# A two-layer transformer kernel on one core: layer 0's values in one visit a group, their parts one step later, rows' transposes behind the sixth scores

## The reference, cut to what matters

```python
x = x + tanh(g_xattn[0]) * L0_xattn(layernorm(x), ctx_768, ...)   # 16 heads x 64, 154 keys
x = x + tanh(g_ffn[0])   * L0_ffn(layernorm(x), ...)              # 8 experts, top 2
x = x + tanh(g_xattn[1]) * L1_xattn(layernorm(x), ctx_768, ...)   # 8 heads x 128, 308 keys
x = x + tanh(g_ffn[1])   * L1_ffn(layernorm(x), ...)              # coupling network

def _L0_xattn_ref(x, context, Wq, Wk, Wv, Wo, bo):
    q, k, v = heads(x @ Wq), heads(context @ Wk), heads(context @ Wv)
    attn = softmax(einsum('bqhd,bkhd->bhqk', q, k) * scale)
    out = einsum('bhqk,bkhd->bqhd', attn, v).reshape(B, Nq, h * dh)
    return out @ Wo + bo
```

## Time and profile before

| | us |
|---|---|
| median of 3 runs | 925.71 (923.45 to 928.28) |
| the profiled execution | 926.4 |
| its span in the trace | 924.6 |
| PE busy | 881.2 (95%) |
| DVE busy | 513.5 (56%) |
| ACT busy | 511.7 (55%) |
| POOL busy | 374.0 (40%) |

### The profile page before, as it was taken

How to read it: one execution, slowest core, us unless ns; L and a number is a source line. 1 busy time by engine, 2 the same in 40 slices (tenths; PEclk the granted TensorE clock), 3 DMA queues, 4 the chain that set the end, 5 groups by cost and what they waited for, 6 DMA issues and landing times.

```text
span 924.6 us, 20158 instructions
## 1 busy us (share of the span) xinstructions
PE 881.2 (95%) x6773; PEld 764.1 (83%) x6774; DVE 513.5 (56%) x1257; ACT 511.7 (55%) x1450; POOL 374.0 (40%) x530
## 2 busy tenths in 40 slices
PE   6989999999999999999999987999999999999996
PEld 4567777777777779999999986899999999987653
DVE  4534434444445764434434447877777776666466
ACT  4576777777775244443343462655655555552565
POOL 3173444444443234455454551534434443443000
PEclk9999999999999799999999998999999999999998
DMA  9000000420002466777777813000000000000002
GB/s 267 1 1 2 1 1 2 146 72 1 0 2 80 138 240 234 244 245 258 232 262 246 252 61 89 25 23 13 12 23 11 12 1 2 1 1 0 1 1 91
DMA packets 36673, 76.18 MB, mean 82 GB/s; under 512 B 4941, under 2 KB 22721, under 8 KB 36481
## 3 DMA queue, kind: packets, MB, share of 16 engines
q1 hardware_dynamic: 32865, 65.11, 21.6%
q0 software_dynamic: 3744, 10.23, 3.3%
HBM read 66.02 MB, written 9.31 MB: 81 GB/s over the span
## 4 chain that ended last, share of the span: by engine, by line
PE 88%; DVE 4%; DMA 3%; issue 2%; ACT 1%; POOL 1%; SPq 0%; DVEq 0%; POOLq 0%
PE banks L1542 14%; PE banks L546 14%; PE banks L548 13%; PE banks L547 13%; PE banks L584 8%; PE banks L595 7%; PE banks L574 5%; PE banks L444 3%; PE banks L1827 2%; PE banks L515 1%; PE banks L1838 1%; PE banks L1832 1%; PE banks L1820 1%; PE banks L1532 1%; DMA region_a<-in_L_ffn_b 1%
## 5 line engine op out<-in xcount | busy, mean ns | idle before, releaser
L1098 ACT ACTIVATE region_a<-banks,negmax 128x154 f32<-128x154 f32 (+1 forms) x384 | 161.7, 434 | 29.3 <-DVE negmax L890 26.6
L1542 PE MATMUL banks<-region_b,region_a 128*128 128x128 f32 x1248 | 146.7, 276 | 1.5 <-ACT region_b L1578 1.4
L1542 PEld LDWEIGHTS banks<-region_b,region_a 128*128 128x128 f32 x1248 | 142.7, 192 | 3.2 <-ACT region_b L1578 1.7
L1242 POOL TENSOR_TENSOR region_a<-region_a,recip 128x640 f32<-128x640 f32 x64 | 80.3, 1255 | 137.4 <-DVE recip L894 137.4
L1205 POOL TENSOR_TENSOR region_a<-region_a,recip 128x512 f32<-128x512 f32 x64 | 66.7, 1042 | 134.3 <-DVE recip L894 94.9
L890 DVE TENSOR_REDUCE negmax<-banks 128x4 f32<-128x616 f32 (+1 forms) x128 | 100.5, 785 | 26.9 <-PE banks L574 14.2
L1633 DVE SCALAR_TENSOR_TENSOR region_b<-banks,region_a,region_b 128x128 f32<-128x128 f32 x156 | 43.9, 343 | 106.7 <-PE banks L1542 99.6
L584 PE MATMUL banks<-ident,region_a 128*128 128x128 f32 x640 | 95.0, 279 | 3.2 <-DVE pT_low L901 1.6
L584 PEld LDWEIGHTS banks<-ident,region_a 128*128 128x128 f32 x640 | 72.5, 141 | 16.6 <-issue 11.6
L546 PE MATMUL banks<-xT_high,Wq_high 128*128 128x256 f32 x256 | 77.8, 304 | 4.1 <-DVE xT_low L882 2.1
L1080 ACT CAST pT_high<-banks 128x640 fp32r<-128x640 f32 x64 | 44.4, 694 | 64.9 <-PE banks L584 64.9
(11 more groups left out here) (293 smaller groups left out, 2344.5 us busy)
## 6 DMA issues: line engine op xcount, KB each, us to landing
region_a<-in_L_ffn_W SPq DMA_DIRECT2D x39, 1024.0 KB
W<-in_L_ffn_W SPq DMA_DIRECT2D x1, 4096.0 KB, 17.9
W<-y_rows SPq DMA_DIRECT2D x16, 256.0 KB, 2.8
out<-x SPq DMA_DIRECT2D x8, 256.0 KB, 2.2
x<-in_x SPq DMA_DIRECT2D x1, 1536.0 KB, 13.1
region_b<-in_L_xattn_Wq SPq DMA_DIRECT2D x1, 1024.0 KB, 8.7
region_b<-in_L_xattn_Wo SPq DMA_DIRECT2D x1, 1024.0 KB, 13.6
xn_rows<-region_b SPq DMA_DIRECT2D x1, 1024.0 KB, 4.4
```

The source lines that it names most:

```text
L1098: e = act.activation(into, source, ACT.Exp, bias=negmax[:, n % 2, u:u + 1], accum_out=sums[:, n % 2, u:u + 1])
L1242: pool.tensor_tensor(probs1[:, n % 2], probs1[:, n % 2], rc, ALU.mult).then_inc(sem("p_norm"), 1)
L1542: mm = pe.matmul(banks[:, 2 * r + part, m * P:(m + 1) * P], W1[r][:, k, cols], xgT[:, r, k, :], start=(k == 0), stop=(k == DK - 1))
```

## The change

It has four parts.

1. **Layer 0's values** are done for a whole group in even steps only, by the new `pe_group_values`: four halves as before and four **quarters**, which hold the remainders as 64 keys by 64 columns (rows 64u of the array, columns 64i) in place of the padded 128 by 64. The output lies in two banks, `o0_ps`, of which bank 5 also receives the fifth transpose. So the fifth transpose in odd steps waits for `o0_copied`, ScalarE's copy of the values. In an even step the values take the probabilities that were transposed in the same step, and wait for their copy (`pt2_high` of this step, before: of the step before).
2. **The parts of a group's output.** ScalarE copies the values to SBUF (`o0T`) in plain float32, at the place where it made the high part. VectorE makes the high part from `o0T` by a copy with a cast, a new instruction, and then subtracts, both in odd steps directly behind the next step's maxima; before, there was the subtraction alone, in even steps. `pe_pair_out` of layer 0 waits for the parts per two chunks.
3. **The rows' transposes** (`pe_pair_x`), in both layers, stand behind the next scores of step 6 instead of ahead of them. Their high part on ScalarE moves from the end of step 5 to the start of step 6, their low part on VectorE from step 5 to step 6, behind the maxima.
4. **`values(6)`** stands ahead of q(0) instead of behind it, in both layers.

```diff
+        def pe_group_values(pe, g, b):
+
+            V = V0[b].bitcast(F32)
+            for u in range(2):
+                for i in range(2):
+                    pe.matmul(o0_ps[64 * i:64 * i + 64, u, :], V[:, 2 * g + u, 128 * i:128 * i + 64], p0T[:, g % 2, 2 * u + i, :],
+                              start=True, stop=False)
+            for i in range(2):
+                for u in range(2):
+                    rows = slice(64 * u, 64 * u + 64)
+                    mm = pe.matmul(o0_ps[64 * i:64 * i + 64, u, :], V[rows, 2 * g + u, 192 + 64 * i:256 + 64 * i],
+                                   p0T[rows, g % 2, 4, :], start=False, stop=True)
+            mm.then_inc(sem("o2_ps"), 1)
...
             for m in range(5):
+                if m == 4 and groups_copied is not None:
+                    pe.wait_ge(sem("o0_copied"), groups_copied)
                 mm = pe.transpose(probsT_ps[:, m * P:(m + 1) * P], row[:, m * P:(m + 1) * P], ident[:])
...
             for c in chunks:
-                if c == NC - 2:
+                if L is L0 and r == 0 and c % 2 == 0:
+                    pe.wait_ge(sem("o2_sb"), groups_done - (NC - 2 - c) // 2)
+                if L is L1 and c == NC - 2:
                     pe.wait_ge(sem("o2_sb"), L.groups + groups_done)
...
                 def values(n):
                     s = 8 * i + n
+                    if L is L0:
+                        if n % 2 == 0 and not (first and n in (0, 2)):
+                            pe.wait_ge(sem(probs_turned), s)
+                            if not (first and n == 4):
+                                pe.wait_ge(sem("o0_copied"), group + n // 2 - 2)
+                            pe_group_values(pe, (n // 2 - 2) % 4, before if n < 3 else batch)
+                        return
...
                 values(5)
+
+                next_scores(6)
                 if not last:
...
                     pe_pair_x(pe, L)
-
-                next_scores(6)
                 transposes(6)
...
+                values(6)
                 if not last:
                     pe.wait_ge(sem("xt2_sb"), x0 + i + 2)
                     pe_pair_q(pe, L, 0)
-                values(6)
...
             def o_rest(g, group):
                 high, low = oT_parts[L.index]
                 part = slice(2 * g, 2 * g + 2)
+                if L is L0:
+                    dve.wait_ge(sem("o0_copied"), group + 1)
+                    dve.tensor_copy(high[:, part, :], o0T).then_inc(sem("o2_high"), 1)
                 dve.wait_ge(sem("o2_high"), g0 + group + 1)
-                dve.tensor_tensor(low[:, part, :], o_ps.rearrange("p (u n) -> p u n", u=2),
+                dve.tensor_tensor(low[:, part, :], o0T if L is L0 else o_ps.rearrange("p (u n) -> p u n", u=2),
                                   high[:, part, :].bitcast(F32), ALU.subtract).then_inc(sem("o2_sb"), 1)
...
                             row_max((n + 1) % 8, s + 1)
+                    if n == 6 and not last:
+                        pair_x_rest(i + 2)
                     if not (first and n == 0):
                         probsT_rest((n - 1) % 8, s - 1)
+                    if L is L0 and n % 2 == 1 and not (first and n in (1, 3)):
+                        o_rest((n // 2 - 2) % 4, 4 * i + n // 2 - 2)
...
             def o_high(g, group):
                 act.wait_ge(sem("o2_ps"), g0 + group + 1)
+                if L is L0:
+                    if not (isinstance(group, int) and group == 0):
+                        act.wait_ge(sem("o2_sb"), group)
+                    act.copy(o0T, o0_ps).then_inc(sem("o0_copied"), 1)
+                    return
```

More of the change, by code:

```diff
@@ L184, in flamingo @@
         p0T = reg_a.part(10 * PAIR, "p (q m n) -> p q m n", q=2, m=5)
+        reg_a.at += 3 * DC
+        o0T = reg_a.part(2 * PAIR, "p (u n) -> p u n", u=2)
+        assert reg_a.at <= P0_AT + 20 * PAIR
         reg_a.at = P0_AT + 20 * PAIR
@@ L360, in flamingo @@
         o_ps = banks[:, 6, :]
+        o0_ps = banks[:, 5:7, P:P + PAIR]
         misc_ps = banks[:, 7, :]
@@ L579, in pe_pair_scores, with pe_pair_probsT @@
             mm.then_inc(sem("s_ps"), 1)
-        def pe_pair_probsT(pe, L, n):
+        def pe_pair_probsT(pe, L, n, groups_copied=None):
             row = normed if L is L0 else probs_row[:, n % 2]
             for m in range(5):
+                if m == 4 and groups_copied is not None:
+                    pe.wait_ge(sem("o0_copied"), groups_copied)
                 mm = pe.transpose(probsT_ps[:, m * P:(m + 1) * P], row[:, m * P:(m + 1) * P], ident[:])
             mm.then_inc(sem("pt_ps"), 1)
+        def pe_group_values(pe, g, b):
[10 more added lines that the diff above has]
+            mm.then_inc(sem("o2_ps"), 1)
         def pe_pair_pv(pe, L, g, u, b):
             c = 2 * g + u
[L590 to L601, removed]
+            for i in range(3):
+                m = 3 * u + i if i < 2 else 2
+                mm = pe_split(pe, o_ps[:, u * PAIR:(u + 1) * PAIR], (V_high[:, c, i, :], V_low[:, c, i, :]),
+                              (pT_high[:, g % 2, m, :], pT_low[:, g % 2, m, :]), i == 0, i == 2)
             if u == 1:
@@ L665, in transposes @@
                             pe.wait_ge(sem(probs_turned), s - 1)
-                        pe_pair_probsT(pe, L, (n - 1) % 8)
+                        turned = L is L0 and n % 2 == 1 and not (first and n < 5)
+                        pe_pair_probsT(pe, L, (n - 1) % 8, 4 * i + n // 2 - 1 if turned else None)
                 def next_scores(n):
@@ L707, in emit @@
                             pe.wait_ge(sem("l1_low"), len(L1_PARTS))
-                    pe_pair_out(pe, L, 0, misc_ps, range(0, 4), None)
+                    pe_pair_out(pe, L, 0, misc_ps, range(0, 4), 4 * i)
                 values(2)
@@ L761, in pe_pairs @@
             pe.wait_ge(sem(probs_turned), STEPS - 1)
-            pe_pair_probsT(pe, L, 7)
+            pe_pair_probsT(pe, L, 7, GROUPS - 2 if L is L0 else None)
             if L is L0:
@@ L765, in pe_pairs @@
                 pe_rows(pe, 2)
-            pe_pair_pv(pe, L, 2, 1, b)
+            if L is L0:
+                pe.wait_ge(sem(probs_turned), STEPS)
+                pe_group_values(pe, 2, b)
+            else:
+                pe_pair_pv(pe, L, 2, 1, b)
             if L is L1:
@@ L772, in pe_pairs @@
             pe.wait_ge(sem(probs_turned), STEPS)
-            pe.wait_ge(sem("o2_sb"), g0 + GROUPS - 1)
-            for u in range(2):
-                pe_pair_pv(pe, L, 3, u, b)
+            if L is L0:
+                pe.wait_ge(sem("o0_copied"), GROUPS - 1)
+                pe_group_values(pe, 3, b)
+            else:
+                pe.wait_ge(sem("o2_sb"), g0 + GROUPS - 1)
+                for u in range(2):
+                    pe_pair_pv(pe, L, 3, u, b)
             if L is L1:
@@ L1011, in emit @@
                         add_y(dve, L, 2 * i + n // 2 - 3, n // 2 - 1, misc_ps[:, 0:D])
-                    if n == 5 and not last:
-                        pair_x_rest(i + 2)
                     if n > 5 and not last and L is L1:
                         pair_q_rest(4 * i + n - 1, n - 6)
-                    if n % 2 == 0 and not (first and n in (0, 2)):
+                    if L is L1 and n % 2 == 0 and not (first and n == 0 or first and n == 2):
                         o_rest((n // 2 - 2) % 4, 4 * i + n // 2 - 2)
@@ L1147, in emit @@
                     s = 8 * i + n
+                    if n == 6 and not last:
+                        x_high(i + 2)
                     if not (first and n == 0):
@@ L1153, in emit @@
                         pair_q_high(4 * i + n + 3, n + 2)
-                    if n == 5 and not last:
-                        x_high(i + 2)
                     if n > 5 and not last:
```

2 lines of the change are left out of this document (added).

## The result

The changed kernel takes 948.26 us (942.95 to 951.29, four runs) against 924.75 for the kernel before: the ratio is 1.0231, interval 1.0197 to 1.0265. It is slower by 2.3%, on the side that was forecast, and 11 us above the 937 given: outside the forecast's own 930 to 945 and inside the wide range of 919 to 949 by 0.7 us only. A second measurement of the same file, among the experiments, gave 943.79 against 926.04, 1.0194 (1.0161 to 1.0227). The profiled execution took 942.95, 16.6 more than that of before.

A forecast was written before the change was run, and what follows sets the result against it. TensorE was taken as the bound (busy 95% of the span). Terms -14.4 - 0.5 - 5.1 + 3.8 + 6.0 + 11.9 + 5.8 + 2.2 + 1.3 = +11.0 on 926.4 gave about 937 us; own range 930 to 945, wide 919 to 949.

The forecast's parts named there:

- values, 4 groups: Layer 0's values on TensorE: a group takes 1.98 us instead of 2.44, -14.4 us over 32 groups.
- (a): Layer 0, values(6) directly behind T(6) wait for ScalarE's copy of these transposes: +0.64 x 6 = +3.8 us.
- (b): Layer 0, T(7)'s fifth transpose waits for ScalarE's copy of the values, behind the q copy: +1.0 x 6 = +6.0 us.
- (c): Layer 0, step 3: chunk 6 of the rows' output waits for VectorE's parts: 1.7 x 7 pairs = +11.9 us.
- (d): Layer 0, step 5: rows' transposes wait for y_done, late on VectorE: +0.97 x 6 = +5.8 us.
- (e): Odd steps: q copies no longer covered between block and next scores: +0.18 at two places a pair, +2.2 us.
- -0.85 x 6 = -5.1: Layer 1: moved rows' transposes and values(6) save waits of 0.71 + 0.25, less 0.11 kept back, in us.
- the prediction's upper case: In (c), S being scores' start: blocked cast ends S+2.9, subtraction S+3.4 to 4.0; wait +1.4 to +2.0 us.
- The row at 43.94: Normalisation begun 0.08 ahead of GpSimd's product, taking 1.27 us against 0.38 alone; cited as evidence that GpSimd locks VectorE.
- rival one: VectorE is not held by GpSimd: (c) 0.85 x 7, (d) 0.15 x 6; 926 us, no change; chance 0.28.
- rival two: Parts in layer 0 are done when chunk 6 comes; (c) and (d) both gone gives 919 us; chance 0.10.
- rival three: Quarters run two at a time: values term +13.8 instead of -14.4; 965 or 951 us; chance 0.10.

The follow-up runs named there:

- the run with the copy first: Changed kernel with ScalarE's copy of layer 0's values ahead of the copy of q(0) in step 6: 940.45 us, ratio 1.0151.

## Why the prediction was right, and where not

What was right is the way it went: layer 0's values won almost what was worked out, the five waits named took more than that back, and the sum of a pair came out above zero. What a pair of layer 0 shows, term by term, is in the table. The measured sizes are those of the pair from 125.34 to 159.57: the interval between two neighbouring matmul starts of the trace, less the interval that the same kinds of neighbours have where nothing is waited for.

| term, us a pair of layer 0 | predicted | measured | worked out as |
|---|---|---|---|
| values, 4 groups | -1.80 | -1.68 | 4 x (2.44 - 2.02) |
| (a) values(6) behind T(6) | +0.64 | +0.61 | 1.05 - 0.20, less the 0.24 for xT_low that went |
| (b) T(7)'s fifth transpose | +1.0 | +0.89 | 1.00 - 0.11 |
| (c) chunk 6 in step 3 | +1.7 | +1.43 | 1.55 - 0.12 |
| (d) y_done | +0.97 | +0.62 | 0.84 - 0.22 |
| (e) q copies | +0.37 | +0.23 | one place in place of two: 0.24 + 0.22 - 0.03 - 0.20 |
| transposes of step 2, behind GpSimd | none | +0.16 | 0.38 - 0.22 |
| rows' transposes, other changes of shape | -0.09 | +0.02 | the rest |
| whole pair | +2.8 | +2.28 | 34.23 - 31.95 |

The row that I had not listed is the contention's other side: GpSimd's slowed products end late, and the next transposes wait for them. No row shows the 0.09 that the prediction allows for a semaphore; in (a) the copy ends at 127.27 and the values start at 127.32, so 0.05. The layer's seven intervals are 13.7 longer; its terms came to 16.1 with the first pair and the tail.

**The term that failed is layer 1**, "-0.85 x 6 = -5.1". It counted the two waits that go, for x and for xT_low, and kept back 0.11 as a choice for what comes late. What comes late is a whole chain: values(6), moved ahead of q(0), no longer lies between q(0) and the scores that need it. One pair after the change:

```profile
670.72 0.58 ACT L1109 CAST q_high<-banks 128x512 fp32r<-128x512 f32 x1 [0.83 <-PE banks L552]
```

```profile
671.33 0.69 DVE L906 TENSOR_TENSOR q_low<-banks,q_high 128x512 fp32r<-128x512 f32 x1 [1.18 <-ACT q_high L1109]
```

```profile
672.08 0.41 PE L550 MATMUL banks<-K_high,q_high 128*128 128x308 f32 x1 [0.85 <-DVE q_low L906]
```

High part, low part, 0.85 idle on PE. In layer 0 I had asked what comes late behind q(0) (terms (b) and (e)); in layer 1 not. With 0 in its place the sum is +16.1, so 942.5 on the scale of the profiled execution, which took 942.95. That this is so close is partly luck: layer 0's terms were some 2 too large together, and layer 1's last pair, which had no wait for x to win, lost 0.75, and the clock around the experts and at the end adds a few us of either sign. The median of the first measurement is 5 us above its own profiled run, and the three runs above it have lower mean clocks (0.975 to 0.982 against 0.985); the second measurement's median is 1 below its profiled run. So these 5 go with the clock of that set of executions and with no step of the argument.

**Inside (c) the size was nearly right and its parts were not.** I had the cast blocked by the product until S+2.9 and the subtraction slowed a little. The cast began 0.08 ahead of the product and took 0.42, its time alone by the prediction's lower bound; the subtraction took twice its time, 1.41 for 0.69. The parts are ready at S+3.4 (112.31 to 115.73), the near end of the prediction's upper case, so the size came out by another way than the one forecast, and that is luck in part. The row at 43.94, on which I had put the block, also began 0.08 ahead of a product and was held; the casts that began so were not.

Of the Trainium skill's rule ("SBUF — State Buffer", Who interferes with whom) this case shows both halves. On two SBUF inputs: the subtraction takes 0.693 apart from GpSimd and 1.41 behind its product; with one input in PSUM, before, it once took 0.692 with GpSimd at work beside it for 0.51 (62.22). On a cast: in step 7 the order of VectorE's cast and GpSimd's x_biased is turned round between two traces. First the run with the copy first, then the changed kernel:

```profile
98.83 0.74 POOL L1230 TENSOR_TENSOR x_biased<-x,gated_bo 128x256 f32<-128x256 f32 x1
...
99.02 0.84 DVE L939 CAST o0T_high<-region_a 128x512 fp32r<-128x512 f32 x1
```

```profile
99.37 0.41 DVE L939 CAST o0T_high<-region_a 128x512 fp32r<-128x512 f32 x1
...
99.38 0.99 POOL L1228 TENSOR_TENSOR x_biased<-x,gated_bo 128x256 f32<-128x256 f32 x1
```

Each took longer where it began second: the cast 0.84 for 0.42 (six times in that run), x_biased 0.99 for 0.74. The subtraction does the same. Once in the changed kernel it begins 0.04 ahead of the product, keeps its 0.69, and the product takes 1.55 for 1.04 (a normalisation, line 1312, lies beside its last 0.6, so a part may be due to that):

```profile
300.63 0.69 DVE L941 TENSOR_TENSOR o0T_low<-region_a,o0T_high 128x512 fp32r<-128x512 f32 x1
...
300.67 1.55 POOL L1245 TENSOR_TENSOR region_a<-region_a,recip 128x512 f32<-128x512 f32 x1 [2.01 <-PE banks L590]
```

So the block that I had looked for exists, and in these rows the one that begins second is held. In step 3 the cast came first by 0.08 and the subtraction came second. The row at 43.94, which came first and was held all the same, doesn't fit, and why is open.

One sign that I had set for rival one did appear: a cast of about 0.4 that ends before the product does; and the cast of over 0.6, a sign of being right, didn't appear beside the product of step 3. The sign didn't tell the two apart, since the time went into the subtraction. Rival one would have needed the subtraction at 0.69 beside the product, rival two both operations in a third of their time, rival three a visit of over 2 us; lines 939, 941 and 603 exclude them. Of the chances, the parts add up to 0.17 faster and 0.63 slower, 0.01 off the totals given.

## What to carry to other kernels

When a step is moved ahead to cover one wait, list everything that it used to stand in front of: values(6) covered q(0)'s two copies, and ahead of q(0) it covered only the parts of x. A shorter stream on the bounding engine is worth its difference only if what the other engines make for it is ready when it falls due; the same values in one visit took 1.0194 or 0.9953 of the time of the kernel before, by the order of three instructions on VectorE and ScalarE alone. Before a wait is hidden, look at what stands ahead of the work that is waited for: add_y moved by two instructions won what the larger change in layer 1 did not.

## What the runs showed of the hardware that was not expected

A VectorE subtraction with both inputs in SBUF, 128 x 512, takes 0.693 us alone and 1.41 where it began 0.37 behind a GpSimd product, and it slows GpSimd's products too, from 1.04 to 1.23 (with the cast) and from 0.40 to 0.84. In these rows the one that begins second is held: begun 0.04 ahead, the subtraction took 0.69 and the product 1.55. A cast of the same size took 0.42 where it began 0.08 ahead of a product, 0.43 with none beside it, and 0.84 where it began 0.19 behind one. The quarters' time had been forecast, but no row before had shown it: four matmuls with 64 rows and 64 columns of the array start their eight passes within 0.28 us, where the four halves, with 128 rows and 64 columns, need 0.70 (1.08 less 0.38), and from the last start in one shape to the first in the next it is about 0.3.
